# Field-pair products on one core: which DMA brings the left-out rows of x

## What is computed

```python
xi = x[:, pi, :]
xj = x[:, pj, :]
proj = jnp.einsum('bpd,pod->bpo', xi, W)
return proj * xj
```

## Time and profile before

| What | Value |
|---|---|
| median of three runs | 677.53 us |
| the profiled execution's own time | 679.33 us |
| its span, first to last instruction | 677.5 us |
| TensorE busy | 584.0 us, 86% |
| VectorE busy | 411.9 us, 61% |
| GpSimd busy | 402.7 us, 59% |
| ScalarE busy | 205.2 us, 30% |
| moved by DMA | 285.20 MB, mean 421 GB/s |
| mean granted TensorE clock | 0.92 |

### The profile page before, as it was taken

How to read it: one execution, slowest core, us unless ns; L and a number is a source line. 1 busy time by engine, 2 the same in 40 slices (tenths; PEclk the granted TensorE clock), 3 DMA queues, 4 the chain that set the end, 5 groups by cost and what they waited for, 6 DMA issues and landing times.

```text
span 677.5 us, 7040 instructions
## 1 busy us (share of the span) xinstructions
PE 584.0 (86%) x2704; PEld 367.3 (54%) x2704; DVE 411.9 (61%) x528; ACT 205.2 (30%) x257; POOL 402.7 (59%) x242
## 2 busy tenths in 40 slices
PE   6999897989979799797989979799797988979930
PEld 4565554646556465554646556465554646556520
DVE  1777484766847467484756738567384765747630
ACT  3333332333323143231323323233232333323210
POOL 0859466674846658365674846748466673756620
PEclk9999898998989999797998979899797997979985
DMA  8999999999999999999999999999999999999995
GB/s 333 398 425 427 438 437 425 436 425 436 425 436 437 418 435 418 438 435 419 442 413 436 418 432 445 413 432 426 429 435 415 439 418 437 426 421 435 415 424 248
DMA packets 16016, 285.20 MB, mean 421 GB/s; under 512 B 2112, under 2 KB 2240, under 8 KB 4224
## 3 DMA queue, kind: packets, MB, share of 16 engines
q1 hardware_dynamic: 13616, 270.28, 93.8%
q0 software_dynamic: 2016, 13.76, 4.8%
q10 hardware_dynamic: 368, 0.98, 0.4%
HBM read 25.89 MB, written 260.05 MB: 422 GB/s over the span
## 4 chain that ended last, share of the span: by engine, by line
DMA 56%; PE 32%; DVE 7%; issue 1%; ACT 0%; DVEq 0%
DMA out_dram<-staged 56%; PE proj L327 27%; DVE staged L377 7%; PE proj L305 4%; DMA ident_sb<-ident_dram 1%; PE proj L350 1%; ACT x_t L267 0%; DVEq L139 0%
## 5 line engine op out<-in xcount | busy, mean ns | idle before, releaser
L327 PE MATMUL proj<-w_sb,x_t 64*128 64x512 f32 (+7 forms) x2432 | 550.9, 556 | 60.8 <-DVE staged L377 59.4
L377 DVE TENSOR_TENSOR staged<-proj,x_sb 128x1024 f32<-128x1024 f32 (+7 forms) x528 | 411.9, 827 | 240.4 <-PE proj L327 161.5
L252 POOL TENSOR_TENSOR staged<-staged,x_sb 128x1024 f32<-128x1024 f32 (+4 forms) x224 | 387.9, 1752 | 216.5 <-ACT staged L293 215.8
L327 PEld LDWEIGHTS proj<-w_sb,x_t 64*128 64x128 f32 x2432 | 335.8, 197 | 272.1 <-issue 125.1
L293 ACT ACTIVATE staged<-proj 128x1024 f32<-128x1024 f32 (+4 forms) x224 | 172.9, 787 | 407.6 <-PE proj L327 342.3
L267 ACT ACTIVATE x_t<-proj 128x1024 f32<-128x1024 f32 x32 | 31.0, 1021 | 34.7 <-PE proj L305 34.7
L235 POOL DMA_INDIRECT x_sb<-x_dram,rows_sb x14 | 14.5, 1037 | 30.7 <-DVE staged L377 19.7
L305 PE MATMUL proj<-ident_sb,x_sb 128*128 128x128 f32 x256 | 31.8, 278 | 0.0
L305 PEld LDWEIGHTS proj<-ident_sb,x_sb 128*128 128x128 f32 x256 | 28.2, 142 | 5.1 <-issue 5.1
L350 PE MATMUL proj<-ident_sb 128*128 128x128 f32 x16 | 3.7, 425 | 5.5 <-DMA ident_sb<-ident_dram 5.5
L350 PEld LDWEIGHTS proj<-ident_sb 128*128 128x128 f32 x16 | 3.3, 226 | 5.5 <-DMA ident_sb<-ident_dram 5.5
## 6 DMA issues: line engine op xcount, KB each, us to landing
out_dram<-staged SPq DMA_DIRECT2D x14, 4896.0 KB, 25.5
out_dram<-staged SPq DMA_DIRECT2D x14, 3936.0 KB, 29.6
out_dram<-staged SPq DMA_DIRECT2D x14, 3776.0 KB, 27.7
out_dram<-staged SPq DMA_DIRECT2D x14, 3264.0 KB, 25.9
out_dram<-staged SPq DMA_DIRECT2D x2, 1952.0 KB, 16.1
out_dram<-staged SPq DMA_DIRECT2D x2, 1824.0 KB, 21.2
out_dram<-staged SPq DMA_DIRECT2D x2, 1728.0 KB, 22.5
out_dram<-staged SPq DMA_DIRECT2D x2, 1696.0 KB, 19.1
```

The lines of the kernel that those rows point to most:

```text
L252: last = nc.gpsimd.tensor_tensor(product, product, x_sb[tile.parity][:, j * dim:(j + n) * dim], ALU.mult)
L327: last = nc.tensor.matmul(proj[b][h][:, at:at + width], x_t[tile.parity][half, i // 2, :], w_sb[half, col:col + width], start=True, stop=True)
L377: last = nc.vector.tensor_tensor(staged_part(item, i, j, n), proj[b][h][:, at:at + n * dim], x_sb[tile.parity][:, j * dim:(j + n) * dim], ...
```

## The change

ScalarE's plain load is taken out. The partitions left out of the big gather are only 12 to 15 (`APART`) in place of 12 to 19, so it carries 124 rows in place of 120. GpSimd issues a second indirect DMA of four rows for these partitions. It stands ahead of step 3 in GpSimd's list, where ScalarE's load stood in ScalarE's; the big gather stays ahead of step 4 and waits for the four rows to have landed. `rows_sb` has 32 columns in place of 16: the first 16 for the big gather, the others with four row numbers each in the partitions 0 to 3.

```diff
-SKIPPED = range(12, 20)
+APART = range(12, 16)
 NO_ROW = 1 << 20
...
-        rows_sb = sb("rows_sb", [P, tiles], U32)
+        rows_sb = sb("rows_sb", [P, 2 * tiles], U32)
...
-            def load_x(tile):
+            def load_apart(tile):
 
                 _, b, use = list(items(Tile(tile.number - 1, 1 - tile.parity, None)))[-1]
 
                 pool.wait_ge(emptied[b][1], use + 1)
                 pool.wait_ge(pool_scaled[group_of[pool_steps[-1]]], tile.number)
+                at = tiles + tile.number + 1
+                nc.gpsimd.indirect_dma_start(
+                    x_sb[1 - tile.parity][APART.start:APART.stop, :], None, x,
+                    bass.IndirectOffsetOnAxis(ap=rows_sb[0:len(APART), at:at + 1], axis=0),
+                    bounds_check=batch - 1, oob_is_err=False).then_inc(x_apart_loaded[1 - tile.parity], 16)
+
+            def load_x(tile):
+
                 to = tile.number + 1
 
-                pool.wait_ge(x_rest_loaded[1 - tile.parity], 16 * (to // 2))
+                pool.wait_ge(x_apart_loaded[1 - tile.parity], 16 * (to // 2))
                 nc.gpsimd.indirect_dma_start(
...
-                    if item == GATHER_BEFORE and not tile.first and not tile.last:
+                    if item == LOAD_BEFORE and not tile.first and not tile.last:
                         if tile.number == 1:
                             pool.wait_ge(rows_loaded, 16)
+                        load_apart(tile)
+                    if item == GATHER_BEFORE and not tile.first and not tile.last:
                         load_x(tile)
...
-            def load_skipped(tile):
...
-                act.wait_ge(emptied[b][1], use + 1)
-                act.wait_ge(pool_scaled[group_of[pool_steps[-1]]], tile.number)
-                row = (tile.number + 1) * P
-                act.dma_start(x_sb[1 - tile.parity][SKIPPED.start:SKIPPED.stop, :],
-                              x[row + SKIPPED.start:row + SKIPPED.stop, :]
-                              ).then_inc(x_rest_loaded[1 - tile.parity], 16)
...
-                    if item == LOAD_BEFORE and not tile.first and not tile.last:
-                        load_skipped(tile)
...
-                            pe.wait_ge(x_rest_loaded[1 - tile.parity], 16 * loads)
+                            pe.wait_ge(x_apart_loaded[1 - tile.parity], 16 * loads)
...
-    rows[SKIPPED.start:SKIPPED.stop] = NO_ROW
+    numbers = np.arange(batch, dtype=np.uint32).reshape(-1, P).T
+    rows = np.full((P, 2 * numbers.shape[1]), NO_ROW, np.uint32)
+    rows[:, :numbers.shape[1]] = numbers
+    rows[APART.start:APART.stop, :numbers.shape[1]] = NO_ROW
+    rows[:len(APART), numbers.shape[1]:] = numbers[APART.start:APART.stop]
```

More of the change, by code:

```diff
@@ L164, in field_pair_project @@
         x_loaded = [sem(f"x_loaded{h}") for h in range(2)]
-        x_rest_loaded = [sem(f"x_rest_loaded{h}") for h in range(2)]
+        x_apart_loaded = [sem(f"x_apart_loaded{h}") for h in range(2)]
         w_loaded = [sem(f"w_loaded{c}") for c in range(len(w_cuts) - 1)]
@@ L268, in turned_out @@
                         "p k b -> p (k b)"), proj[b][h][:], ACT.Copy).then_inc(emptied[b][h], 1)
-            def load_skipped(tile):
-                _, b, use = list(items(Tile(tile.number - 1, 1 - tile.parity, None)))[-1]
-                act.wait_ge(emptied[b][1], use + 1)
-                act.wait_ge(pool_scaled[group_of[pool_steps[-1]]], tile.number)
-                row = (tile.number + 1) * P
-                act.dma_start(x_sb[1 - tile.parity][SKIPPED.start:SKIPPED.stop, :],
-                              x[row + SKIPPED.start:row + SKIPPED.stop, :]
-                              ).then_inc(x_rest_loaded[1 - tile.parity], 16)
             def emit(tile):
                 for item, b, use in items(tile):
-                    if item == LOAD_BEFORE and not tile.first and not tile.last:
-                        load_skipped(tile)
                     if item == "turn":
@@ L401 @@
         w[h * dim:(h + 1) * dim, :halves[h].shape[1]] = halves[h]
-    rows = np.arange(batch, dtype=np.uint32).reshape(-1, P).T.copy()
-    rows[SKIPPED.start:SKIPPED.stop] = NO_ROW
+    numbers = np.arange(batch, dtype=np.uint32).reshape(-1, P).T
[3 more added lines that the diff above has]
+    rows[:len(APART), numbers.shape[1]:] = numbers[APART.start:APART.stop]
     arrays = {
```

## The result

The changed kernel took 687.53 us, median of four runs (687.29 to 688.25), against 677.53 us. The ratio is 1.0146, with a 95% interval of 1.0125 to 1.0167: slower by 1.5%, where 672 us was forecast. The profiled execution took 687.43 us, its span is 685.6 us (677.5 before; the profiled execution before was 1.8 us slower than its median, so the spans are only 8.1 us apart).

A forecast was written before the change was run, and what follows sets the result against it. Full DMA engines, paced by the most loaded one, were taken as the bound. Balance gave -5.6 us and the other terms nothing, so the median of 677.53 became 671.9, rounded 672; range 669 to 685.

The forecast's parts named there:

- The relief of two engines: DMA engines of the partitions left out of the gather: one loses its relief; nothing to 1.0 us a tile, taken nothing.
- The prediction's own sign of being wrong: A single DMA engine's lag grows faster than before, a tile of 41 us or more; or GpSimd's wait holds the chain.
- The other relieved engine is a slow one: Rival, chance 0.20: the DMA engine losing its relief is slow and sets the pace; 41.3 us a tile, +7, time 683.
- deciding point of 0.77 us a tile: Slowness of the DMA engine losing its relief, against the others, above which the prediction let that rival decide.
- The ninth row: ScalarE's row on each of eight DMA engines goes away: 0.4 us a tile gained, taken -5.6 us over 14 tiles.
- The second gather and GpSimd's new wait: On GpSimd: four rows land after 8.4 us, big gather goes out 4.7 us later, wait near 5 us; no time added.
- TensorE's cover: Ahead of the turn: TensorE's new wait of about 2 us comes out of its 3.5 us waits for slot 3.
- 1 us of cover is left: What remains of TensorE's wait for slot 3 after its new wait, with the tile at 40.3 in place of 40.77.

The follow-up runs named there:

- kernel with 16 to 19: The changed kernel with partitions 16 to 19 set apart in place of 12 to 15: 677.22 us, ratio 0.9987.
- kernel with both edits: The changed kernel with partitions 16 to 19 set apart and the gather of four rows ahead of GpSimd's step 0: 672.29 us, ratio 0.9922.
- ScalarE, 16 to 19: The kernel before with only partitions 16 to 19 left out of the gather and loaded by ScalarE: 678.80 us, ratio 1.0019.

## Why the prediction was wrong

**The step that failed** is "The relief of two engines", which was "taken nothing". Its other end, "1.0 us a tile is added to it", was the case. For "nothing" the slow engine had to be the first of the two, or none; it is the second, which takes the partitions 16 to 19. Its own slowness is about 1.1 us a tile, and with 8 rows it needs about 41.2 us, as every kernel shows that leaves it unrelieved (41.02 to 41.28). The prediction's own sign of being wrong held: a single engine's lag, and a tile of 41 us or more.

The rival "The other relieved engine is a slow one" named this mechanism, with a chance of 0.20. Its tile was right, 41.3 us for the measured 41.28. Its time wasn't: by its own +7 us it should have been 684.5 and not 683, and nothing was added for the end of the run, where another 3 us lie (below). Its deciding point of 0.77 us a tile doesn't follow from its terms either: an engine with 8.25 rows needs 37.8 + 8.25 x 0.31 = 40.36 us, so over 0.41 us of slowness it passes 40.77.

The tiles alone don't make the time. Of the 8.1 us between the two spans, the eleven tiles between the turns make 6.3, and 3.1 lie behind the last of these turns (113.8 us to the end, 110.7 before); the changed kernel was 1.3 ahead at the first. The kernel with 16 to 19 has nearly the same tile (41.13) and a span 9.2 us shorter; its advantage, too, lies mostly at the end: from the turn at 571.86 the changed kernel has 113.8 us to go, the other, from 570.70, 105.7. The kernel with both edits, which has neither limit, has 110.5 us to go from 559.88. So the changed kernel needs 3.3 us more, which fits the slow engine's backlog of about 10 us that has still to be worked off. The one with 16 to 19 needs 4.8 us less, which fits a limit in the gather of the next x: it holds the turns back and ends with the last gather. Both of these are readings; no run took them apart.

**The ninth row** was sized too small. With 15 engines level and the slow one relieved, the tile fell by 0.61 us (40.70 to 40.09) where 0.4 was taken. With ScalarE's four rows in place of the second gather (ScalarE, 16 to 19) the tile is 40.84, 0.75 us over 40.09. If all of this is the ninth row on four engines, it costs more than twice its own 0.31 us. But the two kernels differ also in the queue that brings the four rows and in the place of the issue, and no run here takes these apart.

**The second gather and GpSimd's new wait** were right in place and size: 8.6 us to landing for 8.4, the big gather 4.4 us later for 4.7, GpSimd's wait 6.2 us for about 5. The Trainium skill's 2.0 us for the fixed part of such a DMA ("DMA: Bandwidth & Descriptors", Anatomy of one DMA) is not what a DMA behind full queues takes here; the measured 8.6 us decides.

**TensorE's cover** was wrongly reckoned. "1 us of cover is left" took the gather's issue as fixed and let it be late once a tile. But it stands in a ring. The chain of the changed kernel in order of time, from one gather of four rows to the next:

```profile
462.76 8.79 DMA x_sb<-x_dram,rows_sb
...
472.34 17.44 DMA x_sb<-x_dram,rows_sb
489.79 0.04 issue
489.83 1.97 PE proj L302 x16
491.80 6.68 PE proj L324 x34
...
498.57 1.03 ACT staged L290
...
499.67 1.88 POOL staged L262
...
501.99 2.09 POOL staged L262
504.08 0.18 issue
504.26 8.46 DMA x_sb<-x_dram,rows_sb
```

The four rows land, the big gather lands, the turn runs, TensorE does the rest of the tile and the next tile's first steps, ScalarE and GpSimd follow with the steps 0 and 1, and behind these GpSimd issues the next four rows: 41.5 us in this tile with almost no slack. What TensorE waits for in one tile, it hands on to the next gather; nothing takes it in. Before, ScalarE issued its load at 129.90 and the next at 168.82, and in between the ring had 7.2 to GpSimd's gather, 18.1 to its landing, 2.9 of slack, and 10.7 from the turn at 158.09: 36.0 us of work. The change made the ring longer: from the issue of the four rows to that of the big gather it takes 9.6 us in place of 7.2, and from the turn to the next issue 14.4 in place of 10.7, now that the issue stands on GpSimd's list behind the steps 0 and 1; the big gather itself took 0.7 less. That makes just about the length of the slow engine's tile. So the one limit hides the other, and neither edit alone beats the kernel before. With the four rows ahead of step 0 the ring is free again: in the kernel with this edit alone the big gather lands at 568.11 and the turn starts at 571.69, 3.6 us later.

**Shown and not shown.** Shown by pairs that differ in one line: which rows are relieved decides 10 us without and 14 us with the early gather; the place of the gather 1 us without and 5 us with the relief. Read from the packets of all ten traces: that it is this engine's store rows that are slow. In the slot 2 stores 7 to 9 of 128 rows (median store) are slow in every kernel. They are mostly the last to end in the six kernels that leave 16 to 19 wholly or half unrelieved (38 to 49 of the 56 last-four rows), and hardly ever in the four that relieve all of them (0 to 5 of 56). What makes it slow isn't known. The gathers don't: in a first-tile piece with rows of 12,544 bytes, stored before any gather, 6 to 8 of the 128 rows are slow in all ten traces. It isn't slow in every store either: with 16 to 19 set apart and the gather not moved, most of the later slot 1 stores have no slow row.

## What to carry to other kernels

Where the DMA engines are full, find out whether they finish a transfer together: count the completion packets in a short window late in the run, and look which store they belong to. Here 15 was one slow engine and 9 an uneven load; the relief had to go to exactly the slow engine. When a wait is said to be covered, follow it once around, through what it delays to the next issue of the same instruction; in a ring only the ring's own slack counts. And if an edit that takes away one limit brings nothing over the old kernel, look for a second limit of the same length before giving it up.

## What the runs showed of the hardware

One DMA engine moved store rows of 38 KB in about 1482 ns on average of the four read, where the others took 1448 ns, in the same transfer. It was so on both chips that the experiments ran on. Setting apart the partitions 16 to 19 relieves it, 16 and 17 about half as much, 12 to 15 and 20 to 23 not at all; so in the gather these four neighbouring partitions go to one engine, and their neighbours on both sides don't. That is what the Trainium skill gives in "DMA: Bandwidth & Descriptors" (The descriptor swizzle): by its formula, given for one transfer to all 128 partitions, 12 to 15 belong to engine 3, 16 to 19 to engine 4, 20 to 23 to engine 5. The runs, with an indirect DMA, agree on these groups. The Trainium skill, on the same page (Latency and other measured facts), says that the engines 7 and 15 are usually the slow ones; by the swizzle it would be number 4 here, and the measurement decides. The trace has no engine numbers, so 4 is an inference from that formula.

A gather of four rows leaves far more packets than rows. In 132.5:141.5 of the changed kernel q0 has 32 packets for it, 4 rows and 28 small ones:

```profile
q0 software_dynamic: 32, 0.03, 1.0%
```

They took no time that shows: with them and with the slow engine relieved, the DMA engines are level and the tile is the shortest of all.
